# Fill keys with distinct zero rows, one-hots stored edge by edge, three histogram tiles to a projected one, and a later place for the unused-slot matmuls

## The reference

```python
xn = layernorm(x)
# graph convolution: the degree counts the edges into a node that are no self-loops, plus one
deg = segment_sum(w_cnt, fdst); dinv = rsqrt(deg)
gnn = segment_sum((dinv[fsrc] * dinv[fdst] * w_cnt)[:, None] * (xn @ W)[fdst], fsrc)
# linear attention, 8 heads of 32, with elu(.) + 1 as the feature map
q, k = fmap(xn @ wq + bq), fmap(xn @ wk + bk); v = xn @ wv + bv
mix = (q @ (k.T @ v)) / (q @ k.sum(0) + 1e-6) @ wo + bo        # for each head
x = x + gnn + mix
# 8 experts of 256 x 1024 x 256, each token goes to its two best
x = x + sum over the two of weight * expert(layernorm(x))
```

## Time and profile before

| | |
|---|---|
| three runs, us | 2425.78, 2419.67, 2429.38 (median 2425.78) |
| the profiled execution, us | 2423.19 |
| its span, us | 2421.4 |
| mean granted clock | 0.964 |
| busy, us | PE 2176.5, DVE 1228.0, ACT 1156.3, POOL 1365.6 |

### The profile page before, as it was taken

How to read it: one execution, slowest core, us unless ns; L and a number is a source line. 1 busy time by engine, 2 the same in 40 slices (tenths; PEclk the granted TensorE clock), 3 DMA queues, 4 the chain that set the end, 5 groups by cost and what they waited for, 6 DMA issues and landing times.

```text
span 2421.4 us, 50709 instructions
## 1 busy us (share of the span) xinstructions
PE 2176.5 (90%) x11974; PEld 1741.6 (72%) x11975; DVE 1228.0 (51%) x2160; ACT 1156.3 (48%) x2830; POOL 1365.6 (56%) x1379
## 2 busy tenths in 40 slices
PE   2999999888899999999999995768999999999998
PEld 1667776676666666666666663328999999999997
DVE  8897885566666666666666665453212222222221
ACT  4564224666666666666666663922223223233232
POOL 3524770777777777777777773003454454454453
PEclk9999789999999999999999999858999999999999
DMA  4000003333333333333333346537666666666663
GB/s 150 1 17 12 4 4 120 105 106 104 106 105 105 105 104 106 104 105 105 105 105 104 106 118 67 186 124 242 190 174 181 186 175 183 184 176 186 180 177 77
DMA packets 135355, 290.30 MB, mean 120 GB/s; under 512 B 28452, under 2 KB 76768, under 8 KB 135171
## 3 DMA queue, kind: packets, MB, share of 16 engines
q0 software_dynamic: 68736, 140.65, 24.3%
q1 hardware_dynamic: 66563, 149.00, 18.8%
HBM read 253.61 MB, written 34.37 MB: 119 GB/s over the span
## 4 chain that ended last, share of the span: by engine, by line
PE 66%; issue 8%; DVE 8%; DVEq 7%; POOL 7%; DMA 2%; ACT 0%; ACTq 0%; POOLq 0%; SPq 0%
PE B L1596 16%; PE B L1492 15%; PE B L1605 15%; POOL BIG L513 7%; PE B L1376 5%; DVE ACC L559 4%; PE B L1416 3%; DVEq L888 3%; PE B L1393 2%; PE B L1385 2%; PE B L1382 2%; DMA BIG<-table,W2A 2%; DVEq L880 2%; PE B L1565 2%; PE B L1465 1%
## 5 line engine op out<-in xcount | busy, mean ns | idle before, releaser
L513 POOL DMA_INDIRECT BIG<-table,W2A x848 | 801.8, 946 | 309.6 <-issue 226.0
L559 DVE TENSOR_TENSOR ACC<-ACC,B 128x512 f32 x848 | 583.2, 688 | 406.0 <-PE B L1492 296.8
L1161 ACT ACTIVATE BIG<-B,SMALL 128x128 f32<-128x128 f32 (+1 forms) x889 | 251.1, 387 | 531.8 <-PE B L1596 531.8
L1492 PE MATMUL B<-BIG,W2A 128*128 128x256 f32 x1696 | 417.7, 390 | 77.0 <-DVE ACC L559 50.6
L1492 PE MATMUL B<-BIG 128*128 128x256 f32 x1696 | 414.7, 389 | 46.9 <-DMA BIG<-table,W2A 19.2
L1492 PEld LDWEIGHTS B<-BIG,W2A 128*128 128x128 f32 x1696 | 291.8, 189 | 179.5 <-issue 152.6
L1492 PEld LDWEIGHTS B<-BIG 128*128 128x128 f32 x1696 | 300.2, 190 | 153.1 <-issue 112.6
L1596 PEld LDWEIGHTS B<-BIG,W1A 128*128 128x128 f32 x3360 | 396.0, 194 | 6.7 <-DVE BIG L562 1.4
L1596 PE MATMUL B<-BIG,W1A 128*128 128x128 f32 x3360 | 396.7, 277 | 1.0 <-DVE BIG L562 1.0
L1605 PE MATMUL B<-W2A,BIG 128*128 x1680 | 380.1, 379 | 0.7 <-DVE BIG L559 0.7
L533 POOL DMA_INDIRECT out_dram<-BIG,SMALL x105 | 170.5, 1623 | 343.5 <-DVE BIG L562 343.5
(11 more groups left out here) (249 smaller groups left out, 2058.4 us busy)
## 6 DMA issues: line engine op xcount, KB each, us to landing
W1A<-in_w SPq DMA_DIRECT2D x105, 1024.0 KB, 6.6
BIG<-table,W2A POOLq DMA_INDIRECT x848
W2A<-in_w SPq DMA_DIRECT2D x1, 8192.0 KB, 28.1
token_x<-BIG SPq DMA_DIRECT2D x24, 256.0 KB, 2.1
out_dram<-ACC SPq DMA_DIRECT2D x1, 6144.0 KB
W2A<-in_x SPq DMA_DIRECT2D x1, 3584.0 KB, 12.9
table<-ACC SPq DMA_DIRECT2D x2, 1792.0 KB, 7.7
W2A<-in_x SPq DMA_DIRECT2D x1, 2560.0 KB
```

What stands on the lines that cost most here:

```text
L513: pool.indirect_dma_start(G[h][:, u, :], None, table, bass.IndirectOffsetOnAxis(ap=dst_T[:, c:c + 1], axis=0)).then_inc(gath[h][u // 2], 16)
L559: return dve.tensor_tensor(o, a, b, op)
L1161: return nc.scalar.activation(o, i, fn, **kw)
L1492: last = mm(B[u][:, k * D:(k + 1) * D], OH[h % 2][:, u, k * P:(k + 1) * P], G[h][:, u, :], start=True, stop=True)
```

## The change

- The 190 fill keys that are never needed get different sources (6400 + 4 k + lane) and one of the 256 zero rows as destination. POOL makes the first numbers with an iota at the start, DVE the keys while the list totals are on their way; the fill slots proper are handled as before, on 50 columns instead of 240.
- `oh_lo` and `oh_hi` are stored edge by edge: the digits of one edge lie next to each other, where the 16 edges of a digit did.
- HG is 3, so HIST_END becomes 45.
- DVE no longer waits for the experts' list ahead of `slot_digits`.
- `last_end` is worked out earlier (ahead of the gates' copy), and PE's unused-slot matmuls stand after slot 1's first product, ahead of slot 2's inputs and slot 0's second product.

```diff
-HG = 4
+HG = 3
...
-        oh_lo = [grid(W1A, S1 + s * 1416, P, HB, BF16) for s in range(2)]
-        oh_hi = [grid(W1A, S1 + s * 1416 + HB * P // 2, NT, HB, BF16) for s in range(2)]
+        oh_lo = [grid(W1A, S1 + s * 1416, HB, P, BF16) for s in range(2)]
+        oh_hi = [grid(W1A, S1 + s * 1416 + HB * P // 2, HB, NT, BF16) for s in range(2)]
...
+            ch.add(pool.iota(spare_src, pattern=[[LANES, KEYS - EC - FILLS * NGR]], base=PAD, channel_multiplier=0))
...
-                digits = B[7][:, 0:P].unsqueeze(2)
-                tt(oh_lo[s], lo.to_broadcast([P, P, HB]), digits.to_broadcast([P, P, HB]), ALU.is_equal)
-                tt(oh_hi[s], hi.to_broadcast([P, NT, HB]), digits[:, 0:NT, :].to_broadcast([P, NT, HB]), ALU.is_equal).then_inc(oh_ready, 1)
+                digits = B[7][:, 0:P].unsqueeze(1)
+                tt(oh_lo[s], lo.to_broadcast([P, HB, P]), digits.to_broadcast([P, HB, P]), ALU.is_equal)
+                tt(oh_hi[s], hi.to_broadcast([P, HB, NT]), digits[:, :, 0:NT].to_broadcast([P, HB, NT]), ALU.is_equal).then_inc(oh_ready, 1)
...
             dve.sem_inc(counts_ready, 1)
+            ch.link(ts(spare_src, spare_src, lane, ALU.add))
+            ch.link(ts(spare_dst, spare_src, GN - 1, ALU.bitwise_and))
+            ch.add(ts(spare_dst, spare_dst, float(NT * P), ALU.add))
+            ch.add(ts(spare_src, spare_src, CODE, ALU.logical_shift_left))
+            ch.sync()
+            ch.link(tt(spare_dst, spare_dst, spare_src, ALU.bitwise_or))
+            ch.add(ts(keysI[0][:, EC + FILLS * NGR:KEYS], spare_dst, FLAG, ALU.bitwise_or))
             dve.wait_ge(lists_ready, 1)
...
-            dve.wait_ge(slot_e_out, 16)
             for g in range(PICKS // PC):
                 slot_digits(g, g % 2)
...
             dve.wait_ge(gates_T_ps, 1)
+            ch.link(ts(last_end, exp_tiles, 0.0, ALU.is_gt))
+            ch.link(tt(last_end, last_end, exp_i, ALU.mult))
...
-                    last = mm(B[5][:, 0:NT], oh_lo[s][:, :, b], oh_hi[s][:, :, b], start=False, stop=False)
+                    last = mm(B[5][:, 0:NT], oh_lo[s][:, b, :], oh_hi[s][:, b, :], start=False, stop=False)
...
             inputs(1, 1)
+            first_product(1, 1)
             pe.wait_ge(spare_ready, 1)
             for e in range(E):
                 last = mm(B[5][:, 2 * e:2 * e + 2], reached[:, e, :], ones_2, start=True, stop=True)
             last.then_inc(spare_ps, 1)
-            step(0, 0)
+            inputs(2, 2)
+            second_product(0, 0)
```

More of the change, by code:

```diff
@@ L81 @@
 SWAP_FROM = (1, 0, 1)
-assert len(EARLY) == len(SWAPS) and HG == 4 and HIST_END < NT - 1 and CT_DVE % 7 == 0
+assert len(EARLY) == len(SWAPS) and HG <= 4 and HIST_END < NT - 1 and CT_DVE % 7 == 0
+assert PAD % GN == 0 and PAD + LANES * (KEYS - EC) < 1 << CODE and GN <= 2 * P
 assert KEYS >= EC + FILLS * NGR and CPAD * RPC >= NROWS * P and 4 * P >= NBK * (RPC - 1)
@@ L222, in gps_layer @@
         fill = piece(W2A, S2 + KEYS, KEYS - EC)
+        spare_src, spare_dst = (piece(W1A, S1 + 1400 + 220 * k, KEYS - EC - FILLS * NGR, I32) for k in range(2))
         lane_cols = [piece(SMALL, 1200 + k, 1) for k in range(14)]
@@ L634, in onehots @@
                 when(dve, tk_v, oh_free, t - 1)
-                lo = lo_of[:, bass.ds(t * HB, HB)].unsqueeze(1)
-                hi = hi_of[:, bass.ds(t * HB, HB)].unsqueeze(1)
-                digits = B[7][:, 0:P].unsqueeze(2)
-                tt(oh_lo[s], lo.to_broadcast([P, P, HB]), digits.to_broadcast([P, P, HB]), ALU.is_equal)
-                tt(oh_hi[s], hi.to_broadcast([P, NT, HB]), digits[:, 0:NT, :].to_broadcast([P, NT, HB]), ALU.is_equal).then_inc(oh_ready, 1)
+                lo = lo_of[:, bass.ds(t * HB, HB)].unsqueeze(2)
+                hi = hi_of[:, bass.ds(t * HB, HB)].unsqueeze(2)
+                digits = B[7][:, 0:P].unsqueeze(1)
+                tt(oh_lo[s], lo.to_broadcast([P, HB, P]), digits.to_broadcast([P, HB, P]), ALU.is_equal)
+                tt(oh_hi[s], hi.to_broadcast([P, HB, NT]), digits[:, :, 0:NT].to_broadcast([P, HB, NT]), ALU.is_equal).then_inc(oh_ready, 1)
             def input_stats(first, last):
@@ L691, in _ @@
             ch.add(ts(t0[:, 0:NGR], iota[:, 0:NGR], -1.0, ALU.mult, float(NGR), ALU.add))
-            ch.add(dve.memset(fill[:, FILLS * NGR:KEYS - EC], float(NGR)))
             ch.sync()
@@ L697, in _ @@
             ch.link(ts(fill[:, 0:FILLS * NGR], fill[:, 0:FILLS * NGR], -1.0, ALU.mult, float(NGR), ALU.add))
-            ch.link(ts(keysI[0][:, EC:KEYS], fill, float(GN * ((1 << CODE) + 1)), ALU.mult))
-            ch.link(ts(keysI[0][:, EC:KEYS], keysI[0][:, EC:KEYS], FLAG, ALU.bitwise_or))
+            filled = keysI[0][:, EC:EC + FILLS * NGR]
+            ch.link(ts(filled, fill[:, 0:FILLS * NGR], float(GN * ((1 << CODE) + 1)), ALU.mult))
+            ch.link(ts(filled, filled, FLAG, ALU.bitwise_or))
             ch.add(ts(keys[0][:, 0::2], keys[0][:, 0::2], sg01, ALU.mult))
@@ L1119, in _ @@
             ch.add(ts(slots_1, iota[:, 0:ST], 1.0, ALU.add))
-            ch.add(ts(last_end, exp_tiles, 0.0, ALU.is_gt))
             ch.add(dve.memset(ones_2, 1.0))
@@ L1123, in _ @@
             ch.add(ts(offset_f, offset_f, pcol, ALU.subtract))
-            ch.add(tt(last_end, last_end, exp_i, ALU.mult))
             ch.sync()
```

## The result

The changed kernel takes 2379.65 us (median of four runs, 2377.46 to 2382.38) against 2423.82 us (2419.67 to 2429.38) before: a ratio of 0.981, interval 0.980 to 0.983. The forecast was 2376. The profiled execution has a span of 2376.8 us where it had 2421.4, 44.6 less.

| border | before, us | after, us | earlier by | of it in this stage |
|---|---|---|---|---|
| projected tile 30 starts | 215.07 | 212.74 | 2.3 | 2.3 |
| histogram's closing matmul | 377.59 | 363.70 | 13.9 | 11.6 |
| first gather | 422.45 | 393.58 | 28.9 | 15.0 |
| statistics start (the edge sums' end) | 1501.78 | 1462.61 | 39.2 | 10.3 |
| routing's 98 matmuls start | 1591.91 | 1548.39 | 43.5 | 4.3 |

The account below looks back on a forecast made before the run. Bounds: DVE in projection with histogram, mostly POOL's gathers in the edge sums, PE in the experts. Terms -10.4 - 17.4 - 14.3 - 2.9 - 3.0 = -48.0 us from a profiled 2423.2 gave 2376 (chance 0.75), range 2364 to 2400.

Parts of the forecast that it names:

- Order of storage: Histogram one-hots stored edge by edge: a tile costs PE 0.9 us instead of 1.74, DVE keeps 3.11.
- rival 4: Histogram one-hots: DVE pays for the new order, a tile 4.7 us, +74, total 2450; chance 0.04.
- rival 1: Histogram: packing doesn't speed up the tile, PE bounds at 11.8 us a projected tile, total 2407; chance 0.10.
- rival 3: Projection with histogram: the clock stays halved, a tile costs PE about 13.1 us, total 2428; chance 0.05.
- The histogram's end: Projection with histogram, three tiles to a projected one at 9.9 us: ends at 367.2 instead of 377.59, -10.4 us.
- The hand-over: Histogram's end to first gather: three tiles left to project instead of seven, 27.5 us instead of 44.9, -17.4.
- the table's path: Hand-over: table is late next; first part scaled at +5.9, 19.2 us of writing, some 2 of latency, +27.5.
- Fill keys: End of the edge sums: spare keys on different zero rows cut the last gather's DMA from 17.12 to 2.81, -14.3 us.
- rival 2: End of the edge sums: slow gathers aren't the one row's doing, 14.3 us stay, total 2390; chance 0.06.
- The list's wait: Ahead of routing's 98 matmuls: DVE no longer stands 2.88 us waiting for the experts' list, -2.9 us.
- Unused-slot matmuls: Experts' start: PE's 6.61 us idle filled by tile 1's first product; tile 2's inputs then bound, -3.0 us.

Follow-up runs that it names:

- run 3: Kernel before with only HG = 3 (three histogram tiles to a projected one), one-hots still strided: 2413.58 us, ratio 0.995.
- run 7: Changed kernel with the 128-column one-hots (weight load) stored with a step of 16 again: 2381.03 us (one run).
- run 6: Changed kernel with the 49-column one-hots (moving operand) stored with a step of 16 again: 2388.23 us (one run).
- run 5: Changed kernel with the spare keys pointing at sixteen neighbouring zero rows: 2379.50 us (one run).
- run 8: Changed kernel with the wait for the slot list back and the unused-slot matmuls at their old place: 2388.91 us (one run).
- run 12: Changed kernel with only the routing counts' one-hots stored pick by pick: 2384.26 us (one run).
- run 4: Changed kernel with all spare keys reading the one zero row 6272, sources still different: 2390.28 us (one run).
- run 1: Kernel before with the new fill keys alone (strided one-hots, four to a tile, old waits): 2418.79 us, ratio 0.997.
- run 10: Changed kernel, last table part scaled before the read-back wait, third expert tile's inputs before second half of unused-slot work and first tile's outputs: 2380.23 us (one run).
- run 2: Kernel before with only the one-hots stored edge by edge, four histogram tiles to a projected one: 2395.45 us, ratio 0.987.
- run 9: Changed kernel with four histogram tiles to a projected one and SyncE's table writes held until the keys are read back: 2389.69 us (one run).
- run 11: run 10 plus the routing counts' one-hots stored pick by pick: 2379.79 us, ratio to before 0.981.

## Why the prediction was right, and what in it was not

**Order of storage**: right, and the largest part. I put a histogram tile at 0.9 us for PE; it is 0.57. That changed little further, since DVE is the bound: 9.70 us a projected tile against 9.9. The one-hots kept their time, so rival 4 (DVE pays) is refuted here; so is rival 1 (packing doesn't speed up the tile), by run 3 against after. Its price was too high as well: run 3, which is that rival in being, took 10.55 us a projected tile and not 11.8. With the weights alone at a step, 16 pairs cost 0.56 us more (run 7); with the moving operand alone, 1.05 (run 6). The Trainium skill (TensorE: Matmul & The Clock Gate, Weight-path perf modes — Fast Weight Load (FWL) and DoubleRow) has fast weight load take 128 columns packed or strided, and does not speak of the moving operand there. Read as the prediction read it, that the old loads were fast already, this isn't what run 7 shows. The clock did not stay halved (rival 3): the slices of the histogram show 0.8 and more.

**The histogram's end**: forecast 367.2, in the profiled execution 363.70. Of the 3.5 us, 3.0 are 0.2 us less for each of 15 tiles and 0.6 the last one (5.51 us for 6.09). But this end is one of several: in seven runs whose code is the same up to there (but for the zero rows' numbers) it ended between 359.39 and 365.26.

**The hand-over**: forecast 27.5 us, measured 29.9. (The terms 5.9, 19.2 and 2 of the table's path add up to 27.1; and the unpacking, put at 4.5 us, took 3.5, from 383.29 to 386.84.) "What is late next is the table" was right where the histogram ended late enough: 28.5 us in run 6, 29.0 in run 7, 29.1 in run 5, all with the table as the last wait. So the table's path is itself 1.0 to 1.6 us longer than forecast. The step failed in what it left out: GpSimd is still scattering until 368, and the sum gave these scatters no part. VectorE's scaling holds them, and the table writes delay their landing and the read-back, so that the last part is scaled at 386.84, 23.1 us behind the histogram's end and not 21.1. The gather therefore doesn't follow the histogram any more when that ends earlier: ends at 363.70, 363.89 and 365.26 gave gathers at 393.58, 393.76 and 394.33, but ends at 360.96 and 361.99 gave 398.20 and 399.37 (runs with the parts in the order of after). So my two terms, -10.4 and -17.4, were -13.9 and -15.0, and the sum, -28.9 for -27.8, came near by luck in part: with the same code, histograms that ended 2.7 and 1.7 us earlier (runs 8 and 12) brought gathers 4.6 and 5.8 us later.

**Fill keys**: mechanism right (rival 2 refuted by runs 4 and 5), size off: -10.3 for -14.3. The DMA piece did fall from 17.12 to 2.94. But the 848 gathers took 2.5 us longer than before (1061.4 against 1058.9): eight times, every 20.4 us between 1249 and 1391, a gather waits 0.59 to 0.67 us for PE, where before no such wait is over 0.31. Run 4 has them too, so they come with the new keys and not with the rows that these read. Why they arise stays open. The other 1.4 us stand behind the last transfer: from the last gather's issue (1455.03) to the statistics go 7.6 us, 4.7 more than the 2.94 of a landing, where before 20.4 us held 3.3 more than the 17.12. My sum looked only at whether PE had caught up; behind PE's last group (1457.90) VectorE still has four additions to do, one each 1.05 us, until 1462.52. Before, with PE's groups over 3 us apart, there were two.

**The list's wait**: -2.9 forecast, -4.3 measured; run 8 gives 2.55 to the wait itself and 1.4 to the clock in the statistics, which rose earlier in after than there (1.00 against 0.72); it was 0.72 before the change too. These 1.4 us are not the wait's, which comes behind the statistics, and look like luck: run 1, which still has the wait, had the early clock (0.98 in the third 6 us of its statistics), and from their start to the 98 matmuls it took 88.07 us, 2.3 more than after.

**Unused-slot matmuls**: -3.0 forecast, -1.3 at the third first product, 1.4 by run 8. The mis-sized step is "DVE ... then makes tile 2's inputs (0.73)": between the last slot instruction at 1611.12 and these inputs at 1613.41 DVE has 2.07 us of its own, and the first product begins 1.37 us behind them. The code has the load of the tile's expert number in that gap; the trace shows no row for it. PE also begins the second product 1.11 us late and runs it in 5.40 us at a granted clock of 0.69, where the next one takes 3.62, but then it still waits 1.81 us for VectorE. Run 10, which has these inputs ahead of the second half of the unused-slot work, gains 1.7 us there.

Sum: -44.6 for a forecast of -48.0.

## What to carry to other kernels

Where a matmul's operands are read with a step, price both sides: packing made the pairs two to three times as fast, in the histogram mostly by the moving operand, but the engine that writes the packed order must not lose its own rate; here it had none to lose in the histogram and lost half of it in the routing counts. A stage that is made shorter hands its end to whatever runs beside it: look for the queue that ends just behind (128 scatters here) and for what its engine shares with the work that now comes earlier. And fill-up indices should not all point at one row: sixteen rows were enough.

## What the runs showed of the hardware

- While VectorE multiplies two tensors that both lie in SBUF, GpSimd's scatters take up to 3.50 us instead of 0.96 (run 2 and, without any table write, run 9). Beside the one-hots, whose second input is in PSUM, they take 0.96, and so does the direct DMA of the read-back that GpSimd issues beside such a multiplication (374.21 in after, 377.04 in run 2). The Trainium skill (SBUF — State Buffer, Who interferes with whom) says that a VectorE instruction with two SBUF inputs contends with a GpSimd instruction that reads SBUF, and that one with at most one SBUF input, outside the 2-port modes, doesn't. For scatters and one-hots the trace agrees.
- Large writes to DRAM nearly double a read-back of 512 KB beside them: 9.1 us in after and 9.0 in run 10, where VectorE stands idle, against 4.75 with the writes held (run 9).
- 34 gathers of 128 rows each, most reading one row, leave 15.64 us of transfer behind the last issue; with 16 rows it is the ordinary 2.9 (runs 4 and 5).
- VectorE's comparison of two bf16 tensors in SBUF takes 1.09 us for 1,792 elements when the operand that is repeated is repeated in an outer dimension (after), and 2.03 when it is repeated innermost (run 11). With one f32 input from PSUM the order makes no difference: 2,280 and 2,285 ns for 2,048 elements (after and the earlier trace rows).
- With both operands at a step a histogram tile takes the same time at either clock: before, 1.72 to 1.76 us at a granted clock of 0.50 and 1.70 to 1.78 at 1.00. Packed (after), it takes 0.57 to 0.59 us at 1.00 and 0.79 to 0.88 at 0.50 to 0.58.
- The granted clock was 0.50 in the routing counts with strided and with packed operands alike (1546 to 1586 us in after, 1546 to 1594 in run 11), and the pairs took 382 and 188 ns: at the same clock the step makes up half of the strided pair's time.
